# Expert layers of a transformer on one Trainium2 core: the batches in two halves, the second half's routing between the first half's units of work

## The reference

```python
capacity = max(1, int(Sz * CAP_FACTOR / E) + 1)          # 257 of 1024 tokens
scores = jax.nn.softmax(jnp.einsum('bsd,ed->bse', x, router_w), axis=-1)
gate_vals, sel_idx = jax.lax.top_k(jnp.swapaxes(scores, 1, 2), capacity)
tokens = x[b_idx, sel_idx]
h = jax.nn.gelu(jnp.einsum('becd,edh->bech', tokens, w1) + b1[None, :, None, :])
y = jnp.einsum('bech,ehd->becd', h, w2) + b2[None, :, None, :]
out = jnp.zeros_like(x).at[b_idx, sel_idx].add(y * gate_vals[..., None])
```

## Time and profile before

| | |
|---|---|
| time, median of 3 runs | 2201.67 us (2199.74 to 2201.99) |
| the profiled execution: time, span | 2204.54 us, 2202.8 us |
| PE busy | 1782.4 us, 81% of the span |
| DVE busy | 1411.3 us, 64% |
| ACT busy | 1156.9 us, 53% |
| POOL busy | 556.5 us, 25% |
| mean granted clock of TensorE | 0.875 of full speed (2.4 GHz) |

### The profile page before, as it was taken

The page is one execution under the profiler, slowest core; times in us unless marked ns, Lnnn a source line. Parts: engine busy times, 40 slices in busy tenths (PEclk is TensorE's granted clock), DMA queues, the critical chain, the costliest instruction groups (busy, mean ns, idle before and its releaser), DMA issues. The chain is left out here.

```text
span 2202.8 us, 41789 instructions
## 1 busy us (share of the span) xinstructions
PE 1782.4 (81%) x15109; PEld 948.2 (43%) x15109; DVE 1411.3 (64%) x2863; ACT 1156.9 (53%) x2304; POOL 556.5 (25%) x739
## 2 busy tenths in 40 slices
PE   3699999999999615998058999999999996249982
PEld 1256666666664514776031222222222222237751
DVE  4466666666663478441159999999999983584510
ACT  1326666666666200433044888888888884003430
POOL 1022221212121103787640000000000000017886
PEclk9769999999999755899587999999999997558986
DMA  3762644535610102343330000000000000014333
GB/s 107 215 123 47 134 83 81 95 68 98 121 17 2 39 3 78 58 68 49 58 133 26 19 28 17 18 28 17 18 29 16 17 2 20 22 43 86 60 60 63
DMA packets 97483, 124.74 MB, mean 57 GB/s; under 512 B 14696, under 2 KB 57584, under 8 KB 97264
## 3 DMA queue, kind: packets, MB, share of 16 engines
q1 hardware_dynamic: 72336, 104.59, 19.9%
q0 software_dynamic: 24960, 17.68, 6.0%
HBM read 87.17 MB, written 35.95 MB: 56 GB/s over the span
## 5 line engine op out<-in xcount | busy, mean ns | idle before, releaser
L998 DVE TENSOR_REDUCE mx<-wide 128x2 f32<-128x1024 f32 x512 | 603.5, 1221 | 52.5 <-PE wide L930 40.4
L1026 ACT ACTIVATE pT<-bank 128x512 f32<-128x512 f32 x1024 | 555.2, 594 | 85.6 <-PE bank L923 78.1
L747 ACT ACTIVATE pT<-bank 128x512 f32<-128x512 f32 (+3 forms) x768 | 350.3, 490 | 239.2 <-PE bank L617 216.4
L923 PE MATMUL bank<-q_st,k_st 51*128 51x512 bf16 x1024 | 355.3, 387 | 21.4 <-ACT pT L1026 5.4
L930 PE MATMUL wide<-k_st,q_st 48*128 48x512 bf16 x1024 | 352.0, 399 | 24.1 <-DVE mx L998 12.9
L716 DVE TENSOR_REDUCE mx<-wide 128x1 f32<-128x640 f32 (+3 forms) x256 | 258.2, 1022 | 120.1 <-PE wide L627 115.6
L939 PE MATMUL bank<-pT,vst 128*32 128x256 f32 x4096 | 328.3, 392 | 0.1
L627 PE MATMUL wide<-k_st,q_st 120*128 120x512 f32 (+3 forms) x768 | 309.8, 415 | 2.5 <-DVE mx L716 1.0
L617 PE MATMUL bank<-q_st,k_st 122*128 122x512 f32 (+3 forms) x768 | 299.1, 393 | 7.1 <-ACT pT L747 5.1
L923 PEld LDWEIGHTS bank<-q_st,k_st 51*128 51x128 bf16 x1024 | 91.6, 93 | 315.8 <-ACT pT L1026 272.9
L1489 POOL DMA_INDIRECT acc_rows<-yg,idxs x128 | 200.7, 1568 | 52.5 <-issue 38.5
(11 more groups left out here) (225 smaller groups left out, 2012.5 us busy)
## 6 DMA issues: line engine op xcount, KB each, us to landing
q_st<-rope_split SPq DMA_DIRECT2D x72, 256.0 KB
k_st<-rope_split SPq DMA_DIRECT2D x72, 256.0 KB
qk_split<-parts SPq DMA_DIRECT2D x8, 1024.0 KB, 7.6
q_st<-qk_split SPq DMA_DIRECT2D x96, 64.0 KB
k_st<-qk_split SPq DMA_DIRECT2D x96, 64.0 KB
qk_parts<-parts SPq DMA_DIRECT2D x8, 768.0 KB, 4.8
xn_rows<-xn SPq DMA_DIRECT2D x8, 512.0 KB, 3.2
w1b<-in_L_ffn_w SPq DMA_DIRECT2D x16, 256.0 KB, 2.8
```

What stands on the lines that cost most here:

```text
L747: e.activation(pT[:, u % NPB, q0:HALF], bank[u % 2][:, q0:HALF], ACT.Exp, scale=scale).then_inc(s_p, 1)
L923: e.matmul(bank[u % 2][:, :], k_st[at][64 * r:64 * r + KROW, jj, kc * P:(kc + 1) * P], q_st[at][64 * r:64 * r + KROW, jj, J * HALF:(J + 1) ...
L998: e.tensor_reduce(mx[G % 2][:, kh, pair:GH:2, c], wide[w % 2][:, :].rearrange("p (r k) -> p r k", r=2), AX.X, ALU.max).then_inc(s_sf, 1)
L1026: e.activation(pT[:, u % NPB, :], bank[u % 2][:, :], ACT.Exp, scale=scale).then_inc(s_p, 1)
```

## The change

Each expert layer becomes one block, `ffn()`, over two halves of two batches. A class `Router` does for one half (16 chunks, 16 rows of 1024 scores) what `route()` and `choose()` did for all. Its scores stand, after one turn of 128x128, as 128 partitions (8 chunks x 16 rows) x 128 tokens, so no DMA spreads them; each count goes over 128 columns where it went over 256; slot and gate are worked out on 128x128 too, with two small matmuls that add what the chunks ahead hold. Its work is cut into 28 steps, written as generators: one for each of TensorE, ScalarE and VectorE. The first half's routing runs at once (`drain`); the second half's steps stand between the instructions of the first half's experts, four to a unit in the first 7 units (`advance`).

A unit is one expert on one half: 16 units, each with 4 gathers and 4 scatters. The scatters wait for the last unit's scatters of the same batch only. The 257th tokens have no scatter: their rows, after the second weights, are summed over the experts on VectorE (`yl_sum`), and added once, with the bias b2, by the 32 matmuls of each `finish` round into PSUM and VectorE into `x_sb` (`add_bias`), after `acc_rows` has been read back. So the bias is no longer added ahead of the experts, and the last layer's output is written from `x_sb`, after that sum. All 8 experts' weights (4 MB) are read at the start of the layer by two DMAs and stay on chip. The hidden tiles have two PSUM banks where they had four. Loops over experts and digits are written out. In the loading stage there are 16 small DMAs for b2 where there were 4, and some more constants.

The core of the diff:

```diff
-        xn_dram = nc.dram_tensor("xn_rows", [B * T, D], F32, kind="Internal").ap()
...
+        xn_dram = [nc.dram_tensor(f"xn_rows{h}", [2 * T, D], F32, kind="Internal").ap() for h in range(2)]
...
+                    for n in range(2 * NC):
+                        e.dma_start(b2blk[n * NE:(n + 1) * NE, n % 4, :], b2).then_inc(s_b2, 16)
...
+        class Router:
...
+                def reach(at):
+                    for j in range(3):
+                        ins = e.tensor_scalar(self.reached[:, j, :], self.byrow[:, :], at[:, j:j + 1].bitcast(F32), None,
+                                              ALU.is_ge, ALU.add, accum_out=self.count[:, j:j + 1])
+                    ins.then_inc(self.cnt, 1)
+                def take(i):
+                    e.wait_ge(self.tot, PRIME + i + 1)
+                    then(e.tensor_scalar(self.passes[:, :], self.totals[:, 0:3], float(CAP), None, ALU.is_ge, ALU.add,
+                                         accum_out=self.digit[:, :]))
+                    then(e.tensor_scalar(self.taken[:, :], self.digit[:, :], float(1 << (2 * (NDIGIT - 1 - i))), None, ALU.mult))
+                reach(digit_units[:, 0, :])
+                yield
+                for i in range(1, NDIGIT):
+                    take(i - 1)
+                    then(e.scalar_tensor_tensor(self.trials[:, :], digit_units[:, i, :], self.taken[:, 0:1],
+                                                self.found[:, :].broadcast_to([P, 3]), ALU.bitwise_xor, ALU.bitwise_xor))
+                    reach(self.trials)
+                    mark(e.tensor_tensor(self.found[:, :], self.found[:, :], self.taken[:, :], ALU.bitwise_xor))
+                    yield
+                take(NDIGIT - 1)
+                then(e.tensor_tensor(self.found[:, :], self.found[:, :], self.taken[:, :], ALU.bitwise_xor))
...
+                e.tensor_tensor_scan(scan, tie, tie, 0.0, ALU.add, ALU.max).then_inc(self.cnt, 1)
+                yield
...
+            def tensor(self, e):
...
+                yield
+                yield
+                turn(0)
+                yield
+                for q in range(1, 4):
+                    score(q - 1)
+                    turn(q)
+                    yield
+                score(3)
+                yield
+                yield
+                e.wait_ge(self.pr, PRIME + 1)
+                e.transpose(side[:, 0:P], self.prob.rearrange("p c b e -> p (c b e)"), ident[:, :]).then_inc(self.t, 1)
+                yield
+                for i in range(NDIGIT):
+                    e.wait_ge(self.cnt, PRIME + i + 1)
+                    e.matmul(self.totals[:, 0:3], same_row[:, :], self.count[:, :], start=True, stop=True).then_inc(self.tot, 1)
+                    yield
...
+        def ffn(last):
+            two = range(2)
+            w1b, w2b = buf("w1b", [P, NE, HID]), buf("w2b", [P, NE, KH, D])
...
+            def advance(steps, n):
+                if n < NE - 1:
+                    next(steps)
...
+                    e.dma_start(w1b[:, :, :], w1.rearrange("e p h -> p e h")).then_inc(s_w, 16)
+                    e.dma_start(w2b.rearrange("p e k d -> p (e k) d"), w2.rearrange("e (k p) d -> p (e k) d", p=P)).then_inc(s_w, 16)
...
+                    for h in two:
+                        for b in two:
+                            e.wait_ge(s_sc[b], 32 * NE * (h + 1))
+                            e.dma_start(x_rows(2 * h + b), rows_of(acc_dram[h], b)).then_inc(s_back[h], 16)
...
+                    def scatter(n):
...
+                        e.wait_ge(s_yev, PRIME + n + 1)
+                        for b in two:
+                            if n >= 1:
+                                e.wait_ge(s_sc[b], 32 * n)
+                            for m in (2 * b, 2 * b + 1):
+                                e.indirect_dma_start(acc_dram[n // NE], bass.IndirectOffsetOnAxis(ap=idx[n % 4][:, m:m + 1], axis=0),
+                                                     yg[n % 2][:, m, :], None, compute_op=ALU.add).then_inc(s_sc[b], 16)
...
+                    gather(0)
+                    gather(1)
+                    for n in range(UNITS):
+                        if n + 2 < UNITS and (n + 2) % NE >= 2:
+                            gather(n + 2)
+                        scatter(n)
+                        if n + 1 == NE:
+                            gather(NE)
+                            gather(NE + 1)
...
+                    other = half[1].tensor(e)
+                    read_slots(0)
+                    read_slots(1)
+                    for n in range(UNITS):
+                        h, ex = divmod(n, NE)
+                        if n == NE:
+                            read_slots(NE)
+                            read_slots(NE + 1)
...
+                        if n + 2 < UNITS and (n + 2) % NE >= 2:
+                            read_slots(n + 2)
+                        advance(other, n)
...
+                        for k in range(KH):
+                            tile_free(n * TILES + k)
+                            e.matmul(tile_bank[(n * TILES + k) % 2], w1b[:, ex, k * P:(k + 1) * P], xgT[n % 2][:, :],
+                                     start=True, stop=True).then_inc(s_h, 1)
+                        advance(other, n)
...
+                        for k in range(KH):
+                            ins = e.matmul(tile_bank[(n * TILES + KH) % 2][:, k * P:(k + 1) * P], w1b[:, ex, k * P:(k + 1) * P],
+                                           xlT[h][:, :], start=True, stop=True)
+                        ins.then_inc(s_h, 1)
...
+                        for m in range(NMH):
+                            for k in range(KH):
+                                ins = e.matmul(y_ps[:, m * P:(m + 1) * P], hT[:, k, m * P:(m + 1) * P],
+                                               w2b[:, ex, k, :], start=(k == 0), stop=(k == KH - 1))
+                            if m == 1:
+                                advance(other, n)
+                        ins.then_inc(s_y, 1)
...
+                        for k in range(KH):
+                            ins = e.matmul(yl_ps, hl[:, k, :], w2b[:, ex, k, :], start=(k == 0), stop=(k == KH - 1))
+                        ins.then_inc(s_yl, 1)
+                        advance(other, n)
+                        if 11 <= n < 15:
...
+                            finish(0, n - 11)
...
+                    for q in range(4):
+                        finish(1, q)
...
+                    drain(half[0].vector(e))
+                    other = half[1].vector(e)
+                    pick(0)
+                    pick(1)
+                    index(0)
+                    index(1)
+                    pick(2)
+                    for n in range(UNITS):
+                        h, ex = divmod(n, NE)
+                        if n == NE:
+                            pick(NE)
+                            pick(NE + 1)
+                            index(NE)
+                            index(NE + 1)
+                            pick(NE + 2)
+                        advance(other, n)
+                        if n + 2 < UNITS and (n + 2) % NE >= 2:
+                            index(n + 2)
+                        advance(other, n)
+                        if n + 3 < UNITS and (n + 3) % NE >= 3:
+                            pick(n + 3)
+                        advance(other, n)
+                        advance(other, n)
+                        e.wait_ge(s_y, PRIME + n + 1)
+                        if n >= 2:
+                            for b in two:
+                                e.wait_ge(s_sc[b], 32 * (n - 1))
+                        e.wait_ge(s_gk, PRIME + n + 1)
+                        e.tensor_tensor(yg[n % 2][:, :, :], y_ps[:, :].rearrange("p (m d) -> p m d", m=NMH),
+                                        gsl[n % 4][:, :, :].broadcast_to([P, NMH, D]), ALU.mult).then_inc(s_yev, 1)
+                        e.wait_ge(s_yl, PRIME + n + 1)
+                        if ex == 0:
+                            ins = e.tensor_scalar(yl_sum[h][:, :], yl_ps, half[h].own_gate[:, ex:ex + 1], None, ALU.mult)
+                        else:
+                            e.wait_ge(s_ylev, PRIME + n)
+                            ins = e.scalar_tensor_tensor(yl_sum[h][:, :], yl_ps, half[h].own_gate[:, ex:ex + 1], yl_sum[h][:, :],
+                                                         ALU.mult, ALU.add)
+                        ins.then_inc(s_ylev, 1)
+                        if ex == NE - 1:
+                            blocks(h)
+                        if 11 <= n < 15:
+                            add_bias(0, n - 11)
+                    for q in range(4):
+                        add_bias(1, q)
```

849 lines of the change are left out of this document (377 added, 472 removed).

## The result

2114.67 us, median of 4 runs (2114.11 to 2120.64), against 2200.7 us for the kernel before beside it: ratio 0.9615, 95% interval 0.9597 to 0.9634. Forecast: 2105, range 2070 to 2147. The profiled execution is the longest of the four, 2120.64 us (span 2118.6).

The account below looks back on a forecast made before the run. The head was taken as a VectorE chain, the expert stage as following GpSimd. Heads -43.2 - 44.8, stages -5.6 - 6.0, ends -3.2 + 3.7, loading +2.6 from 2204.54 gave 2108.0, as a median 2105; range 2070 to 2147.

Parts of the forecast that it names:

- Head: From a layer's first statistics to its first gather, for 16 chunks: 67.5 us, a fall of 43.2 and 44.8.
- Statistics to normalisation: Start of the head: half of 6.29 us plus 1.80 of small instructions, 4.95 us.
- A score of four chunks: In the head, each of four passes: 0.86 us, a quarter of 3.42, within a pass of 2.85.
- Rounds: Rounds of the choice in the head: counts 0.27 us apart, 2.04 a round, 30.6 for 15.
- Tail, masks and wake-up: End of the head: slots, gates and last token 8 us; masks, indices and GpSimd's wake-up 8.1.
- The first eight units: Expert stage, first gather to GpSimd's first scatter of unit 7: 111.4 us, units 2 to 5 at 12.8 to 13.3.
- the rival of GpSimd deciding from unit 1 on: Expert stage: TensorE keeps 2.4 GHz, 13 us less a layer, 2079, or 2068 with the short head; chance 0.17.
- The stage's second half: Units 8 to 15 of the expert stage, reckoned as GpSimd's own scatters and gathers: 77 us, taken as 78.
- TensorE 7.8 (2.4 GHz): TensorE's work in one expert-stage unit: 7.8 us at 2.4 GHz, 11.9 at 1.2 GHz.
- The gap between the halves: From unit 7 to unit 8, nothing prepared: masks 9 us, gathers and landing 6.5, then the unit: 25.5 us.
- Fully serial: Rival, expert stage: each of four steps adds its 2.04 us to GpSimd's 12.4, 20.6 a unit, 2209; chance 0.03.
- routing after the first half: Rival: second half's routing waits until the first half is through, 57 us a layer less 12, 2195; chance 0.01.

Follow-up runs that it names:

- The last kernel: Changed kernel with units 8 and 9 prepared in unit 7, finish rounds in units 8 to 11, square-root table loaded early: 2089.21 us, ratio 0.949 to the kernel before.
- half the additions: Changed kernel with two scatters a unit instead of four, half of the expert rows left out: 2106.98 us, ratio 0.9584 to the kernel before.
- kernel without hiding: Changed kernel with all 28 second-half routing steps run between units 7 and 8: 2208.83 us, ratio 1.0056 to the kernel before.
- kernel with counts twice: Changed kernel with three more counts a round, into tiles nobody reads: 2153.58 us, ratio 0.9797 to the kernel before.

## Why the prediction was right, and where its sum was off

**Head: 67.5 forecast, 65.8 and 65.7 measured.** Right as a sum, with errors both ways that cancel in part: 1.1 and 2.8 us too little, 0.4, 3.3 and 2.0 too much. The timeline of the first layer:

```profile
749.54 1.28 ACT L1337 ACT_TABLE_LOAD   x1 [7.16 <-DVE lnv L1240]
...
751.38 4.19 DVE L1247 TENSOR_SCALAR xn<-x_sb,lnv 128x128 f32<-128x128 f32 x16
...
754.41 1.87 PE L1362 MATMUL bank<-rwt,xnT 128*128 128x8 f32 x8 [0.69 <-ACT xnT L1343]
...
756.14 1.09 PE L1356 MATMUL wide<-ident,xn 128*128 128x128 f32 x4
...
775.10 0.34 DVE L1272 TENSOR_SCALAR_CACHE_REDUCE reached<-byrow,trials 128x128 f32<-128x128 f32 x1
...
776.27 0.16 DVE L1278 TENSOR_SCALAR_CACHE_REDUCE passes<-bank 128x3 f32<-128x3 f32 x1 [0.21 <-PE bank L1382]
...
776.92 0.35 DVE L1272 TENSOR_SCALAR_CACHE_REDUCE reached<-byrow,trials 128x128 f32<-128x128 f32 x1
```

- Statistics to normalisation: 6.1 for 4.95. ScalarE loads a table between the variance and its square root, 1.28 us, which the forecast had left out. The last kernel took it back.
- A score of four chunks: 1.73 for 0.86. The row of 16 matmuls in 3.42 us is 8 chunks, two instructions to a 32-bit matmul; I took it as 16 chunks. Four times 0.87 is 3.5 us too little. The hand-offs are shorter than taken, so that a pass takes 3.5 us for 2.85 and the four take 14.2 for 11.4. The softmax, its turn and its copy then take 2.8 for 3.2.
- Rounds: 1.82 for 2.04. The counts are 0.27 apart as forecast, but the matmul answers in 0.37 and not in 0.53. 3.3 us too much. That round stands in the range as its lower end.
- Tail, masks and wake-up: 14.1 for 16.1; GpSimd started 0.27 us after the indices and not 0.82.

**The first eight units: 107.1 and 107.7 for 111.4.** For units 2 to 5 the forecast took VectorE at 13.2, the upper of its two ends; the lower, 11.9, is what was measured (11.6 to 12.0). The forecast let the largest of the three engines decide in each unit, and by that GpSimd, at 12.65, would decide there. It does so only for its own rows: with half the additions the eight units take 106.9 and 107.3, so the chain's sum over them is what counts, and the rival of GpSimd deciding from unit 1 on (2079) is out. GpSimd's own time for them, with unit 0's start, is the 99.2 of the kernel without hiding.

**The stage's second half is the step that failed.** The sum had 78 us from unit 8 to 15, as GpSimd's own work; it took 84.8 and 86.2, and it is the chain's work: three units at 10.7, three with a finish round at 12.8 and one at 14.3 are 84.8. The forecast rests on "TensorE 7.8 (2.4 GHz)" a unit and on the sentence that the bias matmuls "run beside GpSimd". The first is the misreading of the scores again: 64 instructions in 7.39 us are 32 matmuls, so 16 second matmuls cost 3.7 us and not 1.85, and the four tiles, priced from the same row at 0.46 each, cost 3.95 together and not 1.85. Half the additions showed the chain at 10.68. The second is wrong in every unit from 11 on: a round adds 2.1 us to the chain, whatever GpSimd does. GpSimd's rows hide it up to unit 13, while it still has gathers; in units 14 and 15 it has 7.4 us of work and waits, 21.3 us from unit 13 to 15 where the sum had 14.9. The gap between the halves is 28.3 and 29.1 for 25.5: masks and landing came as worked out (8.8 and 6.4), but unit 8 took 13.1 for 10, with its four tiles at the lower clock (5.68 us).

In all the stages gained 0.3 and lost 2.1, where 5.6 and 6.0 were forecast to be gained: 13.4 us too little time in the sum, of which the heads give back 3.6. The ends (10.9 for 10.0, 16.0 for 15.3) and loading (1.7 for 2.6) add 0.7, and the untouched attentions 1.7: 12.2 us of span, and the profiled execution is 12.6 us above 2108.0. In the median 3.1 of these fall away, since this execution was the longest of its four. That leaves the miss between 2105 and 2114.67: the gain came from the heads, as forecast, and the stages gave nothing.

**What decides the gain** is shown and not only argued: hidden, the second half's routing costs 8 us a layer, in the open 55 and 54 (kernel without hiding); it costs what the chain of TensorE and VectorE then takes beyond the 99.2 us of that kernel, so doubled counts cost 8.4 more (kernel with counts twice); and taking work from GpSimd gives nothing but the last unit's issue (half the additions). Fully serial was the rival on the slower side, at 2209; that the kernel which hides nothing measured 2208.83 is chance, since that rival puts each step on top of GpSimd's work. The rival that this kernel resembles, routing after the first half, was put at 2195, 45 us a layer above the forecast; 47 and 44 were measured.

## What to carry to other kernels

Hiding one stage's chain in another's units is worth the whole chain only as long as every engine keeps slack over the whole stretch. Add up each engine's time over the stretch from counted instructions, with its own waits, and not the largest of each unit: an engine that falls behind in some units and catches up in others decides nothing, though its rows show no wait there. Then look at the places where it runs out of its own work (the last units, the seam between halves), because there the chain's lead or lag comes out. A seam where nothing is prepared costs a full pipeline fill: preparing two units ahead gave 23 us for a few moved lines. Moving work to another unit of the chain that decides gives nothing.
